# Reciprocal softmax sums repeated by DMA instead of TensorE, and one expert's down products ahead of the output projection

## The chip, the cores and the metric

The kernel runs on one core of a Trainium2 chip. The core has TensorE (PE, matrix products, into PSUM banks), VectorE (DVE), ScalarE (ACT), GpSimd (POOL) and SyncE (SP, which here issues DMAs); DMAs move data between HBM and the on-chip memory SBUF. Each engine runs its own list of instructions in order, and they wait for one another by semaphores. The metric is the device time of one execution in microseconds (us); lower is better. PE's clock has two levels, 1.2 and 2.4 GHz.

## What is computed

Two post-norm transformer layers on 16 sequences ("rows" of the batch) of 256 tokens and 128 features, all float32. In short:

```python
x = layernorm(x + attention0(rmsnorm(x)))   # 16 heads of 64; softmax over 256 keys; output projection + bias
x = layernorm(x + moe0(x))                  # 8 experts (hidden 256), top 2, plus one shared expert
x = layernorm(x + attention1(x))            # 16 tiny heads of 8, attention between the heads of one token
x = layernorm(x + moe1(x))                  # 8 experts (hidden 512), top 2
# attention0, per row of the batch and head:
weights = softmax(q @ k.T * Dh ** -0.5)     # exp(s - max) / sum of exps
out     = (weights @ v) @ w_out + b_out
```

The change concerns the division by the sum of exps in attention0.

## The kernel before

The 16 rows of the batch go through a software pipeline. Iteration `it` does attention0 and the first layer's up projections for row `it` (`v.a`), the rest of layer 0 and attention1 for row `it - 1` (`v.b`), and the second experts' down products and last norm for row `it - 2` (`v.c`). Weights are loaded once. Rows 0 and 1 run with a partly filled pipeline. Iterations 2 to 14 run as a hardware loop on every engine (`run`).

The order on PE is written out by hand in `pe_units`: a list of unit names with the PSUM bank of each. A bank has two semaphores: PE fills it (`v.fill(name)`), and whoever reads it last drains it (`v.drain(name)`); before PE starts a unit it waits until the previous unit of the same bank is drained. Banks S0/S1 take scores, T0/T1 transposed probabilities, A0/A1 alternate over QK, O, HT, OUT, V and X1T, and F0/F1 alternate over the fill units: down products D0p (layer 0) and D1e0 to D1e7 (layer 1, one expert each, 16 products in float32), and some small ones. By that alternation OUT takes the bank of O6, D1e6 the bank of D1e4 and D1e7 that of D1e5.

Attention0 of a row is a loop over 8 head pairs s:
- PE: scores S of pair s + 1, then O of pair s - 1 (values times probabilities, 64 + 64 output rows by 256 tokens), fill units, transposes T of pair s, QK of pair s + 3, fill units. After the loop: O7, the output projection OUT (32 products over all 8 pairs), D1e6, D1e7, V0, X1T (transposes of the normed sum), V1, V2 and the up projections U0 and U1 of the two layers.
- DVE: row maxima of each score bank (`head_max`, L711), the small part of QK (`lower_qk`), mixing of the down products into x (`mix`, L790), head attention of attention1 (L801 to L846), layer norms (L747 to L755), and for the division `inverse_sums` (L719) and `o_scale` (L724).
- ACT: the exponentials with row sums (`softmax_exp`, L573), copies out of PSUM (L552, L566), GELU (L594, L601), and for the division `o_out` (L561) and `repeat_inverse` (L625).
- POOL: norm roots (L446, L447) and half of attention1's products (L479 to L491).
- SP: one load of x (L381) and one store of the output (L421) per row; all weight loads at the start, the last of them (w1 and w2 among them) in `load_late`. w1 and w2 are 2 MB each.

The division: the exponentials' row sums stand one per partition (query token), but O is computed transposed, with tokens along the free dimension. So the reciprocals [128 tokens, 2 heads x 2 token tiles] are repeated by ACT to 64 columns per head (`row_inv`), transposed by PE with the identity into the other half of O's bank (`spread`, 2 transposes per pair), and DVE multiplies ACT's copy of O by them. PE runs `spread(s - 1)` ahead of the scores of pair s + 1, and for the last two pairs ahead of O itself. In `inverse_sums`, `settled` is a drain of the engine's pipeline.

## Time and profile before

| | us |
|---|---|
| median of 3 runs (lowest, highest) | 1432.32 (1432.04, 1434.01) |
| the profiled execution | 1431.51 |
| its span, first to last instruction | 1429.70 |
| PE busy | 1366.9 |
| DVE busy | 925.6 |
| ACT busy | 904.3 |
| POOL busy | 502.5 |
| mean granted PE clock, share of full | 0.988 |

All times in the profile are counted from the start of the span. Lnn is a line of the kernel. Busy time is the sum of the times in which an engine had an instruction in flight. A matmul's recorded duration is its latency in a pipeline, so several overlap; the time from one start to the next, or the piece it has in the chain of work that ended last, tells what it costs. An idle time in square brackets stands ahead of an instruction, with the instruction that released it.

### The profile page before, as it was taken

The numbers are of one execution on the slowest core, as the hardware profiler recorded it, in microseconds if no ns is written. First come the engines' busy times: TensorE is split into PE (matmuls) and PEld (weight loads), VectorE is DVE, ScalarE is ACT, GpSimd is POOL, SyncE is SP. The second block draws the span as 40 slices with busy tenths as digits, with TensorE's granted clock in tenths as the row PEclk, the third lists the DMA queues.
The fourth block names the chain that finished last, engine by engine and source line by source line (L and its number), as shares of the span: only waits on it lengthen the run. The fifth ranks groups of instructions, "written<-read, shape, count | busy, mean of one in ns | idle before, by whom it ended". The sixth has DMA issues, their size and how long they took to land.

```text
span 1429.7 us, 33458 instructions
## 1 busy us (share of the span) xinstructions
PE 1366.9 (96%) x11456; PEld 1202.2 (84%) x11456; DVE 925.6 (65%) x2535; ACT 904.3 (63%) x2492; POOL 502.5 (35%) x409
## 2 busy tenths in 40 slices
PE   6897999999999999999999999999999999999867
PEld 4685989888898988889898898988889898888767
DVE  4366576675766757566675757667576675756684
ACT  6675766757577575766657576675757657575423
POOL 3307062350705316071440706235070531607100
PEclk9999999999999999999999999999999999999988
DMA  7000000000000000000000000000000000000000
GB/s 262 5 1 5 1 2 8 0 7 0 0 7 0 7 0 0 7 0 7 0 7 0 0 7 0 7 0 7 0 0 7 0 7 0 0 5 1 5 1 8
DMA packets 13944, 13.77 MB, mean 10 GB/s; under 512 B 1609, under 2 KB 12754, under 8 KB 13650
## 3 DMA queue, kind: packets, MB, share of 16 engines
q1 hardware_dynamic: 13906, 13.27, 2.9%
q8 instruction: 23, 0.38, 0.1%
q14 instruction: 15, 0.12, 0.0%
HBM read 11.17 MB, written 2.10 MB: 9 GB/s over the span
## 4 chain that ended last, share of the span: by engine, by line
PE 64%; issue 11%; DVE 8%; ACT 4%; DVEq 4%; POOL 3%; POOLq 2%; SPq 1%; DMA 1%; ACTq 0%
PE bank_F L1208 14%; PE bank_S L1081 6%; DVEq L346 4%; PE bank_T L1067 4%; PE bank_T L1122 4%; PE bank_A L1135 4%; PE bank_T L1068 3%; PE bank_T L1069 3%; PE bank_F L1067 3%; ACT probs L573 3%; PE bank_F L1068 3%; PE bank_F L1069 3%; PE bank_A L1146 3%; PE bank_A L1067 3%; PE bank_A L1068 3%
## 5 line engine op out<-in xcount | busy, mean ns | idle before, releaser
L1208 PE MATMUL bank_F<-down,hid 128*128 128x128 f32 x2944 | 357.5, 277 | 5.4 <-DVE x L790 4.6
L1208 PEld LDWEIGHTS bank_F<-down,hid 128*128 128x128 f32 x2944 | 342.0, 192 | 14.7 <-DVE x L790 8.3
L573 ACT ACTIVATE probs<-bank_S,neg_max 128x256 f32<-128x256 f32 x512 | 236.2, 476 | 140.7 <-DVE neg_max L711 140.7
L711 DVE TENSOR_REDUCE neg_max<-bank_S 128x2 f32<-128x512 f32 x256 | 164.6, 684 | 96.1 <-PE bank_S L1081 96.0
L790 DVE SCALAR_TENSOR_TENSOR x<-bank_F,gates,x 128x128 f32<-128x128 f32 x496 | 149.8, 343 | 42.5 <-PE bank_F L1208 32.6
L491 POOL TENSOR_TENSOR hid<-hid,qkv 128x1024 f32<-128x1024 f32 x60 | 169.2, 2831 | 22.6 <-ACT hid L589 22.6
L461 POOL TENSOR_TENSOR mean_sq<-sum_sq,one_over_d 128x2 f32<-128x2 f32 x16 | 3.1, 197 | 442.8 <-ACT h_row L547 442.8
L552 ACT ACTIVATE probsT<-bank_T 128x512 f32<-128x512 f32 x256 | 139.6, 606 | 27.8 <-PE bank_T L1122 27.8
L479 POOL TENSOR_TENSOR hid<-qkv 128x1024 f32<-128x1024 f32 x45 | 121.1, 2690 | 69.3 <-ACT qkv L552 69.3
L1146 PE MATMUL bank_A<-probsT,values 128*64 128x256 f32 x1024 | 139.6, 394 | 1.1 <-ACT probsT L552 1.0
L1122 PE MATMUL bank_T<-ident,probs 128*128 128x128 f32 x1024 | 138.3, 278 | 0.2 <-ACT probs L573 0.2
L1122 PEld LDWEIGHTS bank_T<-ident,probs 128*128 128x128 f32 x1024 | 112.5, 141 | 25.4 <-issue 21.1
L1067 PE MATMUL bank_T<-x1T_hi,up_lo 128*128 128x256 f32 x442 | 129.4, 293 | 0.0
L601 ACT ACTIVATE hid<-bank_T 128x512 f32<-128x512 f32 x141 | 84.4, 598 | 63.6 <-PE bank_T L1069 53.7
L1068 PE MATMUL bank_T<-x1T_lo,up_hi 128*128 128x256 f32 x442 | 123.9, 280 | 0.0
L1069 PE MATMUL bank_T<-x1T_hi,up_hi 128*128 128x256 f32 x442 | 123.8, 280 | 0.0
L446 POOL TENSOR_TENSOR var_eps<-mv,ln_eps 128x2 f32<-128x2 f32 x64 | 12.6, 198 | 303.0 <-DVE mv L749 303.0
L1067 PE MATMUL bank_F<-x1T_hi,up_lo 128*128 128x256 f32 x358 | 103.8, 290 | 3.2 <-DVE x1T_lo L879 2.7
L573 ACT ACTIVATION_READ_ACCUMULATOR probs<-bank_S,neg_max 128x1 f32 x512 | 105.7, 206 | 0.0
L1069 PE MATMUL bank_F<-x1T_hi,up_hi 128*128 128x256 f32 x358 | 100.8, 281 | 0.0
L1068 PE MATMUL bank_F<-x1T_lo,up_hi 128*128 128x256 f32 x358 | 100.7, 281 | 0.0
L486 POOL TENSOR_TENSOR hid<-hid 128x512 f32<-128x512 f32 x75 | 95.3, 1270 | 10.7
(187 smaller groups left out, 3133.2 us busy)
## 6 DMA issues: line engine op xcount, KB each, us to landing
x_row<-in_x SPq DMA_DIRECT2D x16, 128.0 KB, 2.2
hid<-in_w SPq DMA_DIRECT2D x1, 2048.0 KB, 9.1
down<-in_w SPq DMA_DIRECT2D x1, 2048.0 KB, 14.3
out<-x SPq DMA_DIRECT2D x16, 128.0 KB, 1.8
hid<-in_rw SPq DMA_DIRECT2D x1, 1024.0 KB, 7.3
hid<-in_wv SPq DMA_DIRECT2D x1, 512.0 KB, 3.9
hid<-in_wq SPq DMA_DIRECT2D x1, 512.0 KB, 5.1
hid<-in_wk SPq DMA_DIRECT2D x1, 512.0 KB, 5.8
```

The lines of the kernel that those rows point to most:

```text
L479: settled(pool, g.tensor_tensor(prod[:, t, half(i)], q, k, ALU.mult))
L491: ins = g.tensor_tensor(pv1[:, t, half(i)], *weights_and_values(t, i), ALU.mult)
L552: sc.activation(dst, src, ACT.Copy).then_inc(v.drain(name)[0], 1)
L573: ins = sc.activation(probs[:, h // 2 % 2, h % 2, t, :], unit.bank(f"S{h}")[:, t * S:(t + 1) * S], ACT.Exp, bias=neg_max[:, h, t:t + 1], a ...
L711: ve.tensor_reduce(neg_max[:, h, :], v.bank(f"S{h}")[:, :].rearrange("p (t k) -> p t k", t=NT), AX.X, ALU.max, negate=True).then_inc(max_r ...
L790: ins = ve.scalar_tensor_tensor(acc[:, t, :], y[:, j, t, :], gates[i][:, t, e:e + 1], src[:, t, :], ALU.mult, ALU.add)
L1067: te.matmul(out, s_lo, m_hi, start=True, stop=False)
L1068: te.matmul(out, s_hi, m_lo, start=False, stop=False)
L1069: return te.matmul(out, s_hi, m_hi, start=False, stop=True)
L1122: ins = te.transpose(bank[:, k * S + t * P:k * S + (t + 1) * P], probs[:, h // 2 % 2, h % 2, t, tokens(k)], ident[:])
L1146: ins = te.matmul(bank[r, 0:S], values[:, k, s * P + j * DH:s * P + j * DH + DH], probsT[:, j, k, :], start=k == 0, stop=k == NT - 1)
L1208: ins = te.matmul(bank[:, (j * NT + t) * P:(j * NT + t + 1) * P], hid[:, e, k, tokens(t)], down[:, e, k, :], start=k == 0, stop=k == m - 1)
```

## The change

Two things. First, the reciprocals are no longer repeated on ACT and transposed on PE. DVE writes them into a tile padded to 32 columns, transposes it (each 32x32 block by itself), and SP stores the four blocks' first four rows to an HBM buffer `sums_apart` (four DMAs of 4 x 32 numbers), waits for them, and loads each head's row of 256 numbers back, repeated over 64 partitions (two DMAs), into `inv_spread`. DVE then multiplies O's bank by it directly; ACT's copy of O is gone. SP's loop is unrolled, and the loads of w1 and w2 move from SP's queue to ACT's, after ACT's work on pair 0 of row 0. DVE's transpose waits until SP's stores of the pair before have landed; SP's loads wait until `o_scale` of two pairs before is done, and its stores until the loads of the pair before have landed. Second, in PE's list D1e6 moves from behind OUT to ahead of it. DVE's order is the same. Small tiles `var_eps` and `std_inv` are merged into one each. The core of the diff:

```diff
@@ -46,6 +46,7 @@
 SPLIT1 = 8
 FIRST, LAST = 2, ROWS - 2
 LATE = 6
+SQ = 32
@@ -94,8 +95,10 @@
         put("A", f"QK{s + 3}", on=a and s + 3 < HP)
         put("A", "HT", on=nxt and s == HP - 2)
         put("F", *fill_units(it, s, 1))
-    put("A", f"O{HP - 1}", "OUT", on=a)
-    put("F", "D1e6", "D1e7", on=c)
+    put("A", f"O{HP - 1}", on=a)
+    put("F", "D1e6", on=c)
+    put("A", "OUT", on=a)
+    put("F", "D1e7", on=c)
     put("A", "V0", on=nxt)
     put("A", "X1T", on=a)
     put("G", "V1", on=nxt)
@@ -240,8 +243,10 @@
         probs = sb("probs", P, 2, 2, NT, S)
         probsT = sb("probsT", P, 2, NT, S)
         row_sum = sb("row_sum", P, 2, 2 * NT)
-        sum_inv = sb("sum_inv", P, 2, 2 * NT)
-        row_inv = sb("row_inv", P, 2, NT, 2, DH)
+        sum_inv = sb("sum_inv", P, SQ)
+        sum_invT = sb("sum_invT", P, SQ)
+        sums_apart = nc.dram_tensor("sums_apart", [2, 2 * NT, P], F32).ap()
+        inv_spread = sb("inv_spread", P, 2, S)
         oT_early = sb("oT_early", P, HP // 2, S)
         x1 = sb("x1", P, NT, D)
         x1T = split("x1T_hi", P, S), split("x1T_lo", P, S)
@@ -290,8 +295,9 @@
         stats = [sb(f"stats{i}", P, NT, 6) for i in range(4)]
         mv = [sb(f"mv{i}", P, NT, 2) for i in range(4)]
-        var_eps = [sb(f"var_eps{i}", P, NT) for i in range(4)]
-        std_inv = [sb(f"std_inv{i}", P, NT) for i in range(4)]
+        var_eps_all, std_inv_all = sb("var_eps", P, 4, NT), sb("std_inv", P, 4, NT)
+        var_eps = [var_eps_all[:, i, :] for i in range(4)]
+        std_inv = [std_inv_all[:, i, :] for i in range(4)]
         banks = {}
         for n in BANKS:
@@ -312,8 +318,8 @@
         h_ready = sem("h_ready")
         xplus_ready = sem("xplus_ready")
         inverse_ready = sem("inverse_ready")
-        repeated_ready = sem("repeated_ready")
-        o_copied = sem("o_copied")
+        inverse_stored = sem("inverse_stored")
+        inverse_spread = sem("inverse_spread")
         max_ready = sem("max_ready")
         stats_ready = [sem(f"stats_ready{i}") for i in range(4)]
@@ -361,7 +367,8 @@
             return (score1[:, t, half(i)].rearrange("p h (a g) -> p h a g", a=1).broadcast_to(full),
                     qkv1[:, t, :, 2, :].rearrange("p g (a d) -> p a d g", a=1).broadcast_to(full))
-        n_loads = [0] * 5
+        loads1 = (up1_loaded, w1_in), (down1[:], w2_in)
+        n_loads = [0, 0, 0, 0, 16 * len(loads1)]
         def wait_weights(eng, v, group):
@@ -406,8 +413,23 @@
                 load(3, wqkv1[:], wqkv1_in)
                 load(3, wproj[:], wproj_in)
                 load(4, router1[:], router1_in)
-                load(4, up1_loaded, w1_in)
-                load(4, down1[:], w2_in)
+
+            def spread_inverse(v, s):
+
+                sp.wait_ge(inverse_ready, v.at(0, HP, s + 1))
+                if v.it > 0 or s >= 1:
+                    sp.wait_ge(inverse_spread, v.at(0, 32 * HP, 32 * s))
+                for b in range(P // SQ):
+                    block = slice(b * SQ, (b + 1) * SQ)
+                    sp.dma_start(sums_apart[s % 2, :, block], sum_invT[block][0:2 * NT, :]).then_inc(inverse_stored, 16)
+                sp.wait_ge(inverse_stored, v.at(0, 64 * HP, 64 * (s + 1)))
+                if s >= 2:
+                    sp.wait_ge(*v.drain(f"O{s - 2}"))
+                elif v.it > 0:
+                    sp.wait_ge(*v.previous().drain(f"O{HP - 2 + s}"))
+                for j in range(2):
+                    src = sums_apart[s % 2, NT * j]
+                    sp.dma_start(inv_spread[j * DH:(j + 1) * DH, s % 2, :], bass.AP(src.tensor, src.offset, [[0, DH], [1, S]])).then_inc(inverse_spread, 16)
             def body(v):
                 if v.next:
@@ -416,11 +438,15 @@
                     load_x(v.it + 1 + v.step)
                 if v.it == 0:
                     load_late()
+                if v.a:
+                    for s in range(HP):
+                        spread_inverse(v, s)
                 if v.c:
                     sp.wait_ge(ln_ready[3], v.at(2, 1, 1))
                     sp.dma_start(out[v.it - 2 + v.step, :, :].rearrange("(t p) d -> p t d", p=P), x4[:]).then_inc(stored, 16)
-            run(sp, body)
+            for it in range(ROWS + 2):
+                body(Iteration(it, 0, banks))
             sp.wait_ge(stored, 16 * (ROWS + 1))
@@ -432,6 +458,7 @@
             g.affine_select(out=ident[:], in_=ident[:], compare_op=ALU.not_equal, fill=1.0, base=0,
                             pattern=[[-1, P]], channel_multiplier=1)
             g.memset(minus_half[:], -0.5)
+            g.memset(sum_inv[:], 0.0)
             g.memset(table_load[:], 0.0)
             for i in range(2):
                 g.memset(top2[i][:], -3.0e38)
@@ -555,11 +582,6 @@
                 t, half = n // 2, n % 2
                 copy_out(v, f"V{n}", values[:, t, half * 512:half * 512 + 512], v.bank(f"V{n}")[:, :])
-            def o_out(v, s):
-
-                act.wait_ge(*v.fill(f"O{s}"))
-                sc.activation(oT(s), v.bank(f"O{s}")[:, 0:S], ACT.Copy).then_inc(o_copied, 1)
-
             def qk_out(v, s):
                 act.wait_ge(*v.fill(f"QK{s}"))
@@ -618,12 +640,6 @@
                 sc.activation(table_load[:], table_load[:], ACT.Gelu)
                 for u in range(2 * E):
                     gelu1(v, u)
-
-            def repeat_inverse(v, s):
-
-                act.wait_ge(inverse_ready, v.at(0, HP, s + 1))
-                sc.activation(row_inv[:, s % 2], sum_inv[:, s % 2].rearrange("p (j t a) -> p t j a", j=2, a=1).broadcast_to([P, NT, 2, DH]),
-                              ACT.Copy).then_inc(repeated_ready, 1)
             def transposed_probs(v, s):
                 probsT_out(v, 2 * s)
@@ -643,8 +659,6 @@
                     router_exp(v, 1)
                 for s in range(HP):
                     if v.a and s == HP - 2:
-                        o_out(v, s - 1)
-                        repeat_inverse(v, s)
                         transposed_probs(v, s)
                     if v.a and s + 1 < HP:
                         softmax_exp(v, 2 * s + 2)
@@ -652,10 +666,6 @@
                         copy_out(v, "X2T", x2T[:], v.bank("X2T")[:, 0:S])
                     if v.a and s + 1 < HP:
                         softmax_exp(v, 2 * s + 3)
-                    if v.a and s >= 1 and s != HP - 2:
-                        o_out(v, s - 1)
-                    if v.a and s != HP - 2:
-                        repeat_inverse(v, s)
                     if v.b and s == 1:
                         copy_out(v, "WT0", gates0T, v.bank("WT0")[0:E + 1, 0:S])
                     if v.a and s != HP - 2:
@@ -665,14 +675,15 @@
                     if v.b and s == 3:
                         for t in range(NT):
                             copy_out(v, f"LQ{t}", qkv1[:, t].rearrange("p h c d -> p (h c d)"), v.bank(f"LQ{t}")[:, 0:3 * D])
+                    if v.it == 0 and s == 0:
+                        for dst, src in loads1:
+                            act.dma_start(dst, src).then_inc(loaded[4], 16)
                     if v.next and s == 1:
                         squares_of(v)
                     if v.b and s == 5:
                         head_exp(v, 0)
                 if v.b:
                     head_exp(v, 1)
-                if v.a:
-                    o_out(v, HP - 1)
                 sc.activation(table_load[:], table_load[:], ACT.Gelu)
                 if v.next:
                     for n in range(3):
@@ -716,12 +727,16 @@
                 unit = v.previous() if s == 0 else v
                 for j in range(2):
                     dve.wait_ge(*unit.drain(f"S{2 * s + j}"))
-                settled(dve, ve.reciprocal(sum_inv[:, s % 2, :], row_sum[:, s % 2, :]).then_inc(inverse_ready, 1))
+                settled(dve, ve.reciprocal(sum_inv[:, 0:2 * NT], row_sum[:, s % 2, :]))
+                if v.it > 0 or s >= 1:
+                    dve.wait_ge(inverse_stored, v.at(0, 64 * HP, 64 * s))
+                ve.transpose(sum_invT[:], sum_inv[:]).then_inc(inverse_ready, 1)
             def o_scale(v, s):
-                dve.wait_ge(o_copied, v.at(0, HP, s + 1))
-                ve.tensor_tensor(oT(s), oT(s), v.bank(f"O{s}")[:, S:2 * S], ALU.mult).then_inc(v.drain(f"O{s}")[0], 1)
+                dve.wait_ge(*v.fill(f"O{s}"))
+                dve.wait_ge(inverse_spread, v.at(0, 32 * HP, 32 * (s + 1)))
+                ve.tensor_tensor(oT(s), v.bank(f"O{s}")[:, 0:S], inv_spread[:, s % 2, :], ALU.mult).then_inc(v.drain(f"O{s}")[0], 1)
             def lower_qk(v, s):
@@ -1086,14 +1101,6 @@
             def whole_x3T(v):
                 return x3T_late if v.it == ROWS - 1 else x3T[:]
-
-            def spread(v, s):
-
-                bank = v.bank(f"O{s}")
-                pe.wait_ge(*v.drain(f"O{s}", before=1))
-                pe.wait_ge(repeated_ready, v.at(0, HP, s + 1))
-                for t in range(NT):
-                    te.transpose(bank[:, S + t * P:S + (t + 1) * P], row_inv[:, s % 2, t].rearrange("p j e -> p (j e)"), ident[:])
             def unit(v, name):
                 bank = v.bank(name)
@@ -1136,8 +1143,6 @@
                     return ins
                 if name[0] == "O":
                     s = int(name[1:])
-                    if s >= HP - 2:
-                        spread(v, s)
                     for j in range(2):
                         pe.wait_ge(*v.drain(f"T{2 * s + j}"))
                     for k in range(NT):
@@ -1223,8 +1228,6 @@
             def body(v):
                 for name, bank in (pe_units(v.it) if v.it >= 0 else PRE):
-                    if name[0] == "S" and bank == "S0" and v.nth.get(f"O{int(name[1:]) // 2 - 2}"):
-                        spread(v, int(name[1:]) // 2 - 2)
                     free, count = v.drain(name, before=1)
                     if v.it > 0 or count:
                         pe.wait_ge(free, count)
```

## Rows read from the trace of the kernel before

**Rows 1.** The page's first part: busy us, share of the span, instructions, by engine

```profile
PE 1366.9 (96%) x11456; PEld 1202.2 (84%) x11456; DVE 925.6 (65%) x2535; ACT 904.3 (63%) x2492; POOL 502.5 (35%) x409
```

**Rows 2.** Busy us by stage: stretch, its length, PE, PEld, DVE, ACT, POOL, clock

```profile
...
761.00:808.00 47.00, 46.77 (x409) 38.89 (x409) 32.55 (x80) 31.40 (x104) 22.70 (x16) 1.00 0.00 0
...
```

**Rows 3.** Timeline of PE (start, us, line, what), around OUT of a steady row

```profile
...
807.01 0.38 PE L1096 MATMUL bank_A<-ident,row_inv 128*128 128x128 f32 x2
...
808.61 2.05 PE L1135 MATMUL bank_A<-wo,oT_early 128*128 128x128 f32 x16 [0.21 <-DVE hid L724]
...
812.55 3.74 PE L1208 MATMUL bank_F<-down,hid 128*128 128x128 f32 x32
816.05 0.47 PE L1067 MATMUL bank_A<-wv_hi,hT_lo 128*128 128x512 f32 x1
...
816.82 0.38 PE L1051 MATMUL bank_A<-ident,x 128*128 128x128 f32 x2
...
```

**Rows 4.** Timeline of PE, behind OUT of row 15, which has no V0

```profile
...
1320.87 3.74 PE L1208 MATMUL bank_F<-down,hid 128*128 128x128 f32 x32
1324.96 0.41 PE L1051 MATMUL bank_A<-ident,x 128*128 128x128 f32 x2 [0.36 <-DVE x L755]
...
```

**Rows 5.** Instructions on row_inv and oT_early: ns least, median, most; first, last start

```profile
L1096 PE MATMUL bank_A<-ident,row_inv x256: 272/273/328, 24.5 to 1316.0; 128*128 128x128 f32 x128
L625 ACT ACTIVATE row_inv<-sum_inv x128: 404/433/446, 24.0 to 1312.3; 128x256 f32<-128x256 f32 x128
...
L561 ACT ACTIVATE oT_early<-bank_A x64: 392/395/407, 28.4 to 1298.1; 128x256 f32<-128x256 f32 x64
```

**Rows 6.** The chain that ended last (start, us, what), ahead of pair 6's scores

```profile
...
791.07 0.22 PE bank_A L1096 x2
...
```

**Rows 7.** Timeline of DVE in a steady row's attention

```profile
...
761.50 0.17 DVE L719 RECIPROCAL sum_inv<-row_sum 128x4 f32<-128x4 f32 x1
...
795.52 0.17 DVE L719 RECIPROCAL sum_inv<-row_sum 128x4 f32<-128x4 f32 x1
...
798.43 0.53 DVE L831 TENSOR_TENSOR hid<-hid,max 128x256 f32<-128x256 f32 x1
...
802.89 0.18 DVE L719 RECIPROCAL sum_inv<-row_sum 128x4 f32<-128x4 f32 x1 [1.89 <-ACT probs L573]
...
806.91 1.32 DVE L831 TENSOR_TENSOR hid<-hid,max 128x256 f32<-128x256 f32 x1
...
808.48 0.60 DVE L790 SCALAR_TENSOR_TENSOR x<-bank_F,gates,x 128x128 f32<-128x128 f32 x2
...
811.53 0.42 DVE L724 TENSOR_TENSOR hid<-hid,bank_A 128x256 f32<-128x256 f32 x1
...
```

**Rows 8.** DMAs: count, KB each, us to landing; one issue on SP

```profile
x_row<-in_x SPq DMA_DIRECT2D x16, 128.0 KB, 2.2
...
out<-x SPq DMA_DIRECT2D x16, 128.0 KB, 1.8
...
nscale<-in_norm_scale SPq DMA_DIRECT2D x1, 0.5 KB, 2.1
...
741.16 0.39 SPq L421 DMA_DIRECT2D out<-x  x1
```

**Rows 9.** Timeline of POOL beside the second L831 of rows 7

```profile
...
806.68 1.26 POOL L486 TENSOR_TENSOR hid<-hid 128x512 f32<-128x512 f32 x1
...
```

**Rows 10.** The chain that ended last, at the end of row 1's attention

```profile
...
129.03 5.53 POOL hid L491 x2
...
```

**Rows 11.** Row 0: last weight load (chain), DVE's first L719 and last L724

```profile
...
19.77 14.28 DMA down<-in_w
...
20.46 0.18 DVE L719 RECIPROCAL sum_inv<-row_sum 128x4 f32<-128x4 f32 x1 [1.47 <-ACT probs L573]
...
57.84 0.42 DVE L724 TENSOR_TENSOR hid<-hid,bank_A 128x256 f32<-128x256 f32 x1 [1.67 <-ACT hid L561]
...
```

**Rows 12.** Timeline of PE: X1T of row 0

```profile
...
64.64 0.66 PE L1051 MATMUL bank_A<-ident,x 128*128 128x128 f32 x2 [2.80 <-DVE x L755]
...
```

## The prediction

> **What bounds the kernel now.** I read the busy shares first: TensorE (PE) is busy 96% of the span [rows 1], so the question is where its instructions could start earlier. The busy time by stage says the same of one row's attention: 46.77 us of 47 [rows 2]. Then PE's own order of time at the end of that stage: in the stretch of rows 3 it stands still once, for 0.21 us, ahead of the output projection OUT, because VectorE (DVE) has not yet emptied the bank that OUT takes over from O6 [rows 3]. So a steady row (rows 2 to 14 of the batch, and nearly row 15) is PE-bound, but a second chain runs through DVE and ScalarE (ACT) in the last two head pairs and is only 0.2 us behind. After OUT the layer norm of x1 runs on DVE and GpSimd (POOL), and the transposes X1T need it. From the first matmul behind OUT to X1T go 816.82 - 812.55 = 4.27 us, filled by D1e6, D1e7 and V0 [rows 3]. In row 15 only D1e6 and D1e7 stand there, and X1T does wait 0.36 us: 1324.96 - 1320.87 = 4.09 us is what the norm needs [rows 4]. Its cover is thus 0.2 us too long, no more. Row 0 is another regime: its attention isn't PE-bound, and every delay there lengthens the run.
>
> **Parts of the change, on a steady row.**
> (a) `spread` goes: 256 transposes, in 128 pairs [rows 5]. Busy time overstates them (273 ns each); on the chain a pair takes 0.22 us [rows 6]. 8 pairs a row: 8 x 0.22 = 1.76 us of PE, 28 us over 16 rows if nothing else became late. That is the whole prize.
> (b) ACT loses `repeat_inverse` (0.433 us) and `o_out` (0.395 us) on each pair [rows 5]: 0.83 us, wherever ACT sets the pace.
> (c) DVE gains 8 transposes of 128x32 a row. No row shows one. Bounds: the reciprocal of four columns ahead of it, 0.17 us, and the product of 256 columns, 0.42 us [rows 7]. I take 0.2 us, being nearer to the small one. Six of the eight lie in DVE's idle time; two stand in the late chain. Less than nothing is impossible, as nothing is removed from DVE.
> (d) `o_scale` reads the bank directly instead of ACT's copy: same shape, so 0.42 us as before; it is free of ACT but waits for the DMA chain (e).
> (e) The DMA chain on the sync engine (SP) is strictly serial: wait for the reciprocals, four stores, wait for all four, two loads, and the next pair's stores wait for these loads. SP issues a DMA in 0.39 us; a store of 128 KB lands 1.8 us after its issue began, a load of 128 KB after 2.2 us, one of 4-byte pieces after 2.1 us [rows 8]. Stores: three issues of 0.3 to 0.43 us ahead of the last, then 1.6 us (an estimate, 1.8 less a little for the smaller size) to 1.8 = 2.5 to 3.1. Loads: one issue 0.43 ahead, then 2.1 us = 2.5. With 0.2 us for three wakes a round C is 5.2 to 5.8 us; I take 5.4. Bounds from the rows: 2 x 1.8 = 3.6 if all issues overlapped and 4 x 0.43 + 1.8 + 2 x 0.43 + 2.2 = 6.6 if none did.
> What the rounds must meet: the first reciprocal of the row is at 761.50 and `o_scale(7)` at 811.53 [rows 7], 50 us, against 8 x 5.4 = 43.2. There is a second, tighter condition: DVE's transpose for pair s waits until the stores of s - 1 have landed, and queued behind it on DVE are the whole head sums and maxima. For pair 6 (reciprocal at 795.52, about 1.4 us earlier after the change) this asks 761.7 + 5C + 0.53C < 794.1, that is C < 5.85 us. At 5.4 there are 2 us to spare. So in this case the DMA chain costs a steady row nothing; if the cover is gone, it costs 5.5 us per us of C.
> (f) D1e6 moves ahead of OUT. Its bank F1 is that of D1e4, so it can't start before DVE has mixed D1e4 (808.48 + 0.60 = 809.08 [rows 7]), which comes right behind `o_scale(6)`. How much earlier does DVE get there? PE reaches the scores of pair 6 5 x 0.22 = 1.1 us earlier (five spreads lie before). ACT's two instructions no longer stand between head_exp and the exponentials that the reciprocal at 802.89 waits for (1.89 us idle there [rows 7]): 0.6 to 0.8 us more. Against it two DVE transposes, 0.4. So DVE is 1.3 to 1.5 us early. There is a catch in either direction: the same subtraction L831 took 0.53 us at 798.43 and 1.32 at 806.91, ending 0.3 us after a POOL instruction that ended at 807.94 [rows 7, 9]; if it meets the gap between two POOL instructions instead, DVE is up to 2.6 us early. PE itself would be there 1.76 us early. D1e6 then starts 1.0 to 2.0 us before 808.61.
> From there: D1e6 1.75 us (half of 816.05 - 812.55), OUT 812.55 - 808.61 = 3.94, then the norm 4.09 before X1T, of which D1e7 and V0 cover only 1.75 + 0.77 = 2.5 [rows 3, 4]. PE now waits some 1.6 us at X1T. From D1e6's start to X1T 9.78 us, where OUT's start to X1T was 8.21: 1.57 us longer. Net a steady row gains 1.0 - 1.57 = -0.6 to 2.0 - 1.57 = +0.4 us; middle: 0.1 us lost. The 1.76 us that (a) frees turn into a wait at X1T. What D1e6 covers, `o_scale(7)`, which only the last four products of OUT need, wasn't late at C = 5.4. Times 14 rows: +1.4 us (-6 to +8).
> (g) Row 1 has no D1 products and is paced at its end by POOL, whose last two products end 129.03 + 5.53 = 134.56 and hold up the norm's root [rows 10]. POOL's series begins on LQ0, about 1 us earlier than now from three spreads and ACT's relief: -1 us.
> (h) Row 0. Before, 57.84 - 20.46 = 37.4 us from first reciprocal to `o_scale(7)` [rows 11], 4.8 a pair, less than a round. After, 8 x 5.4 = 43.2. Besides, the 4 MB of w1 and w2 go to ACT's queue about 7 us later than now (the last is issued at 19.77 and takes 14.28 us to land [rows 11]) and then cross the small transfers in some two rounds of four to six DMAs; I put 2 to 6 us on that, bounded below by none and above by the 14.28. Hidden: the OUT products before the last four, about 0.5 us. Sum 43.2 + 4 - 37.4 - 0.5 = +9, less 1 since ACT and PE are quicker at the end: +8 us (+2 to +14). POOL's splitting of w1 starts later too, but still ends before the norm.
> (i) Memset, merged small tiles, unrolled SP program: nothing on any chain; SP's waits between rows last tens of us.
>
> **Sum.** +1.4 - 1 + 8 = +8 us on a span of 1429.70. Outside the span lie 1431.51 - 1429.70 = 1.8 us, unchanged; the median of the runs is 0.8 above this execution. 1432.3 + 8 = 1440 us. Its own range by the bounds above: 1427 to 1454.
>
> **Rivals.**
> Rival 1, the DMA rounds set the pace (slower). For it: six issues and two landings of about 2 us are in series, and with the rows' full 0.43 and 1.8 C comes to 5.8 already. Against: the transfers are tiny. It decides from C = 5.85: at 6.2 the transpose of pair 6 stalls DVE 1.9 us, and OUT with it: 14 x 1.6 = +22, row 0 +14, so 1467 us. The Trainium skill (DMA: Bandwidth & Descriptors, Specifications and Anatomy of one DMA) speaks for this rival: pieces below 512 B are read, modified and written, and the receipt from HBM is the heaviest. The stores here are pieces of 128 B into HBM, and no run here shows one; by that rule a store lands later than the 1.8 us row, and the time is this rival's.
> Rival 2, the prize is kept (faster). The norm may be done sooner than row 15 shows, since POOL and DVE are both less loaded ahead of it, and D1e6 may start with PE's full 1.76 us: a row gains 1.2 us, 14 x 1.2 = -17, row 0 +5, row 1 -1: 1419 us. For it: 28 us of PE go, and PE is 96% busy. Against: 4.09 us of norm behind OUT are shown, and only 2.5 of cover stay.
> Rival 3, the clock. PE's transposes x2 took 0.66 us after an idle of 2.80 us in row 0, and 0.38 in a steady row [rows 3, 12]: the lower of its two levels. If the 1.6 us wait at X1T does that in each row, V1, V2 and X1T lose 1.4 us: 14 x 1.4 = +20, so 1460 us. Against: the idle is shorter and PE was full before.
>
> **How the numbers follow.** Forecast 0.50, rival 1 0.22, rival 2 0.20, rival 3 0.08. About 0.2% (2.9 us) is what a measurement can tell. Faster by more: rival 2 nearly whole, and a tenth of the forecast's spread: 0.25. Within: 0.15 of the forecast's half and a little of the rivals': 0.12. Slower: 0.63. For 8 in 10 the range runs from 1419, the centre of rival 2, to 1465, just short of rival 1's centre.
>
> **What would show it.** In the changed kernel's steady row: X1T with an idle of 1 to 2 us on DVE's ln_apply, D1e6 starting when D1e4 is mixed, no wait of `o_scale` for a DMA; reciprocals of row 0 at least 5.4 us apart. SP rounds near 5.4 us confirm (e); above 5.85 the DVE transpose waits for a DMA and rival 1 holds. If X1T doesn't wait, (f) is wrong and rival 2 holds. If row 0's OUT is not several us later, (h) is wrong. Matmuls of double length behind X1T mean rival 3.

## The result and the profile after

The changed kernel takes 1446.8 us (median of 4 runs, 1445.23 to 1447.92), against 1432.18 for the kernel before beside it (4 runs): a ratio of 1.0098, 95% interval 1.0083 to 1.0113. It is slower by 1%. The forecast was 1440.0 with a range of 1419 to 1465. The profiled execution took 1447.92 us, its span is 1446.1 against 1429.70, so 16.4 us are to be explained; mean granted clock 0.979 against 0.988.

The page's first part of the kernel after, to be held against [rows 1]:

```profile
PE 1352.1 (94%) x11200; PEld 1189.6 (82%) x11200; DVE 938.8 (65%) x2663; ACT 827.9 (57%) x2236; POOL 502.2 (35%) x410
```

PE lost 256 instructions and ACT 76 us of work; the time went up all the same. So the reading must go by the clock on the wall, with one mark for each row of the batch: the start of X1T, the transposes of the normed sum, on PE's timeline.

| | X1T of row 0 | row 1 after row 0 | row 2 after row 1 | a steady row | X1T of row 15 | span |
|---|---|---|---|---|---|---|
| before | 64.64 | 71.74 | 86.35 | 84.86 | 1324.96 | 1429.7 |
| after | 78.06 | 72.66 | 84.87 | 84.68 | 1336.60 | 1446.1 |

The 16.4 us are: row 0 +13.4; row 1 +0.9; the 14 rows to row 15's X1T together -2.7; and behind that X1T +4.8, of which 4.1 fall before the next transposes of x on PE (1351.06 against 1335.35).

**A steady row.** PE's timeline around OUT in the kernel after (start us, duration, line; the idle time ahead in brackets), where [rows 3] stood:

```profile
...
817.87 1.08 PE L1151 MATMUL bank_A<-probsT,values 128*64 128x256 f32 x8
818.88 2.05 PE L1213 MATMUL bank_F<-down,hid 128*128 128x128 f32 x16
820.77 1.95 PE L1142 MATMUL bank_A<-wo,oT_early 128*128 128x128 f32 x16
822.56 1.95 PE L1142 MATMUL bank_A<-wo,hid 128*128 128x128 f32 x16
824.34 1.95 PE L1213 MATMUL bank_F<-down,hid 128*128 128x128 f32 x16
826.05 0.48 PE L1082 MATMUL bank_A<-wv_hi,hT_lo 128*128 128x512 f32 x1
...
828.37 0.44 PE L1066 MATMUL bank_A<-ident,x 128*128 128x128 f32 x2 [1.39 <-DVE x L770]
...
```

No spread stands ahead of O7 any more, and D1e6 starts straight behind it. But from D1e7 to X1T go 828.37 - 824.34 = 4.03 us, the norm, and there is work only for the first 2.6: PE waits 1.39 us. This recurs in every steady row. PE's busy time by stage tells the same (stretch, length, then busy us and instructions of PE, PEld, DVE, ACT, POOL, the granted clock, the DMAs' share and GB/s). Before, then after:

```profile
250.00:1200.00 950.00, 944.90 (x8023) 834.39 (x8021) 633.59 (x1773) 626.00 (x1752) 349.69 (x278) 1.00 0.01 3
```

```profile
250.00:1200.00 950.00, 931.10 (x7868) 823.49 (x7867) 638.02 (x1859) 574.83 (x1563) 348.58 (x275) 1.00 0.05 15
```

**The rounds of the DMA chain.** SP's queue in the kernel after: L424 are the four stores, L432 the two loads. First row 0, then a steady row:

```profile
...
21.03 1.28 SPq L424 DMA_DIRECT2D sums_apart<-sum_invT  x4
23.21 1.15 SPq L432 DMA_DIRECT2D inv_spread<-sums_apart  x2
...
35.14 1.89 SPq L424 DMA_DIRECT2D sums_apart<-sum_invT  x4
37.92 1.09 SPq L432 DMA_DIRECT2D inv_spread<-sums_apart  x2
...
774.19 1.27 SPq L424 DMA_DIRECT2D sums_apart<-sum_invT  x4
776.34 1.09 SPq L432 DMA_DIRECT2D inv_spread<-sums_apart  x2
779.51 1.26 SPq L424 DMA_DIRECT2D sums_apart<-sum_invT  x4
...
```

A round is 779.51 - 774.19 = 5.32 us. In row 0 the first one takes 35.14 - 21.03 = 14.1 us: ACT issues the loads of w1 and w2 at 23.30 and 23.73, and pair 0's two loads of `inv_spread`, issued at 23.21 and 23.76, cross these 4 MB and land at 31.02 and 35.07 (w1 lands at 31.80, w2 at 38.12). DVE's waits for DMAs in the kernel after lie nearly all in row 0 (its timeline):

```profile
...
35.16 0.42 DVE L739 TENSOR_TENSOR oT_early<-bank_A,inv_spread 128x256 f32<-128x256 f32 x1 [8.03 <-DMA inv_spread<-sums_apart]
...
37.93 0.21 DVE L733 STREAM_TRANSPOSE sum_invT<-sum_inv 128x32 f32<-128x32 f32 x1 [2.25 <-DMA sums_apart<-sum_invT]
...
```

**Row 15.** It has no V0, and X1T waits 2.48 us instead of 0.36 [rows 4]. PE's timeline in the kernel after:

```profile
...
1336.60 0.41 PE L1066 MATMUL bank_A<-ident,x 128*128 128x128 f32 x2 [2.48 <-DVE x L770]
1338.26 0.55 PE L1082 MATMUL bank_F<-x1T_hi,up_lo 128*128 128x256 f32 x1 [1.25 <-DVE x1T_lo L894]
...
```

Behind it stands a stretch at the lower clock level (columns as above):

```profile
1336.60:1339.60 3.00, 1.75 (x8) 1.55 (x9) 2.69 (x7) 0.00 (x0) 0.00 (x0) 0.64 0.00 0
1339.60:1342.60 3.00, 3.00 (x16) 3.00 (x15) 1.86 (x3) 1.67 (x4) 0.00 (x0) 0.50 0.01 3
...
```

In the kernel before the granted clock is 1.00 in the same place, and 29 matmuls stand in 3 us (1328 to 1331) where 16 stand here.

### The profile page after: what moved, and what is told of

The parts are those of the page before. It is cut to its first block, busy times and chain, and to the rows that moved or that the text cites. A ratio compares the mean times of both kernels' runs of the same rounds, so it can differ in the third digit from the quotient of the medians.

```text
span 1446.1 us, 33731 instructions
## 1 busy us (share of the span) xinstructions
PE 1352.1 (94%) x11200; PEld 1189.6 (82%) x11200; DVE 938.8 (65%) x2663; ACT 827.9 (57%) x2236; POOL 502.2 (35%) x410
## 4 chain that ended last, share of the span: by engine, by line
PE 76%; issue 10%; DVE 5%; POOL 3%; DVEq 2%; POOLq 2%; DMA 1%; ACT 1%; SPq 0%; ACTq 0%
PE bank_F L1213 20%; PE bank_S L1096 7%; PE bank_A L1151 7%; PE bank_T L1129 6%; PE bank_T L1082 4%; PE bank_T L1083 3%; PE bank_T L1084 3%; PE bank_A L1142 3%; PE bank_F L1082 3%; PE bank_F L1083 3%; PE bank_F L1084 3%; PE bank_A L1082 3%; PE bank_A L1083 2%; PE bank_A L1084 2%; DVEq L352 2%
## 5 line engine op out<-in xcount | busy, mean ns | idle before, releaser
L1213 PE MATMUL bank_F<-down,hid 128*128 128x128 f32 x2944 | 361.2, 278 | 5.5 <-DVE x L805 4.6
L518 POOL TENSOR_TENSOR hid<-hid,qkv 128x1024 f32<-128x1024 f32 x60 | 168.9, 2825 | 11.3 <-ACT hid L611 11.3
L1082 PE MATMUL bank_T<-x1T_hi,up_lo 128*128 128x256 f32 x442 | 132.4, 300 | 0.0
L1151 PEld LDWEIGHTS bank_A<-probsT,values 128*64 128x64 f32 x1024 | 63.6, 138 | 49.8 <-DVE oT_early L739 6.8
## 6 DMA issues: line engine op xcount, KB each, us to landing
down<-in_w ACTq DMA_DIRECT2D x1, 2048.0 KB, 14.4
```

The lines of the kernel that those rows point to most:

```text
L518: ins = g.tensor_tensor(pv1[:, t, half(i)], *weights_and_values(t, i), ALU.mult)
L1082: te.matmul(out, s_lo, m_hi, start=True, stop=False)
L1151: ins = te.matmul(bank[r, 0:S], values[:, k, s * P + j * DH:s * P + j * DH + DH], probsT[:, j, k, :], start=k == 0, stop=k == NT - 1)
L1213: ins = te.matmul(bank[:, (j * NT + t) * P:(j * NT + t + 1) * P], hid[:, e, k, tokens(t)], down[:, e, k, :], start=k == 0, stop=k == m - 1)
```

## Experiments

The theory of the forecast, called A below: the DMA chain (5.3 us a round) costs a steady row nothing, taking `spread` away gains, D1e6 ahead of OUT uncovers the norm behind OUT and eats the gain, and row 0 loses by the rounds and by their crossing of the 4 MB.

### The two halves alone

`e1_order_back`, the kernel after with the old order on PE:

```diff
-    put("A", f"O{HP - 1}", on=a)
-    put("F", "D1e6", on=c)
-    put("A", "OUT", on=a)
-    put("F", "D1e7", on=c)
+    put("A", f"O{HP - 1}", "OUT", on=a)
+    put("F", "D1e6", "D1e7", on=c)
```

> The changed kernel with D1e6 behind OUT again, as in the kernel before; the DMA chain stays. Theory A (the order gives back what the removed transposes free): the wait at X1T (1.39 us in a steady row) goes, a steady row takes 83.2 to 83.4 us instead of 84.68, row 15 keeps the high clock (some 4 us), and the median is about 1422 us, below both kernels. Theory B (the DMA chain eats the gain, and D1e6 covers it): OUT's last four products wait for o_scale(7), a steady row takes 84.7 us or more, and the median is 1446 us or higher.

Measured: 1421.92 us, ratio to before 0.9911 (0.989 to 0.9933). A steady row takes 82.9 us. PE's timeline of it around OUT:

```profile
...
808.61 2.05 PE L1140 MATMUL bank_A<-wo,oT_early 128*128 128x128 f32 x16
...
812.28 3.74 PE L1211 MATMUL bank_F<-down,hid 128*128 128x128 f32 x32
...
816.56 0.38 PE L1064 MATMUL bank_A<-ident,x 128*128 128x128 f32 x2
```

OUT follows O7 without a wait, and so does X1T: the norm is covered. The row is 0.3 us shorter than expected, and one part of the expectation failed: row 15 does not keep the high clock (13.39 us from its X1T to the next transposes of x, 10.39 in the kernel before).

`e2_order_alone`, the kernel before with the new order alone (the same lines the other way round):

> The kernel before with D1e6 ahead of OUT, nothing else. Theory A: D1e6 starts when D1e4 is mixed, 0.5 us behind OUT's old start, and X1T follows 9.8 us later instead of 8.2, so a steady row takes 86.5 to 86.9 us instead of 84.87 and the median is 1455 to 1465 us. Theory B: the order costs nothing by itself, 84.9 us a row and 1432 us.

Measured: 1459.13 us, ratio 1.0175 (1.0157 to 1.0194); a steady row 86.8 us. PE's timeline:

```profile
...
823.69 2.05 PE L1210 MATMUL bank_F<-down,hid 128*128 128x128 f32 x16 [0.71 <-DVE x L792]
825.58 1.95 PE L1137 MATMUL bank_A<-wo,oT_early 128*128 128x128 f32 x16
...
833.06 0.44 PE L1053 MATMUL bank_A<-ident,x 128*128 128x128 f32 x2 [1.26 <-DVE x L757]
```

What follows: the two halves pull against each other. The division by DMA takes 84.86 - 82.9 = 1.96 us from a steady row, the new order adds 84.68 - 82.9 = 1.8 (on the kernel before 86.8 - 84.86 = 1.9). Over the whole run the order costs 25 us (1446.8 - 1421.9; 1459.1 - 1432.9 = 26 on the kernel before).

### Is the DMA chain felt in a steady row?

`e4_no_dma`: the kernel after without SP's stores and loads and without the waits for them. `inv_spread` holds a constant, so the division is left out.

```diff
-                if v.a:
-                    for s in range(HP):
-                        spread_inverse(v, s)
...
+            g.memset(inv_spread[:], 0.01)
```

> The changed kernel without the whole DMA chain: no stores, no loads, no waits on them; o_scale multiplies by a constant tile instead of the reciprocals, so the softmax division is left out. DVE still computes and transposes the reciprocals. Theory A: the steady row is the same, 84.6 to 84.7 us, with X1T waiting 1.4 us; only row 0 is shorter, by 13 to 17 us, and the median is 1428 to 1434 us. Theory B: the steady row falls to 83.5 us or less and the median to below 1420.

Measured: 1428.29 us, ratio 0.9955 (0.9939 to 0.997); a steady row 84.70 us with 1.26 us of wait at X1T; X1T of row 0 at 59.94, row 1 70.79. The chain costs a steady row nothing (84.68 with it), 18.1 us in row 0 (a little more than the 13 to 17 expected) and 1.9 in row 1; row 2 gives 2.3 of it back (87.12 against 84.87), which was not followed.

`e7_double_stores`: each store is made twice, the second time into a buffer that nobody reads; eight stores a round.

```diff
+                    sp.dma_start(sums_again[s % 2, :, block], sum_invT[block][0:2 * NT, :]).then_inc(inverse_stored, 16)
...
-                sp.wait_ge(inverse_stored, v.at(0, 64 * HP, 64 * (s + 1)))
+                sp.wait_ge(inverse_stored, v.at(0, 128 * HP, 128 * (s + 1)))
```

> The changed kernel with every store of the reciprocals issued twice (a second HBM buffer takes the extra ones), so that a round takes 6.6 us instead of 5.33; nothing else. The prediction's rival 1 (a round above 5.85 us holds DVE's transpose of pair 6 and with it OUT): a steady row grows by 3.5 to 4.5 us to about 88.7, row 0 by 10, the median is 1500 to 1520 us. If the rounds aren't near any limit: steady rows stay at 84.7, the median is 1457.

Measured: 1538.2 us, ratio 1.0744 (1.0717 to 1.0771); steady rows of 88.9 to 90.8 us, 89.6 on average. SP's queue and DVE's timeline of this run:

```profile
...
829.57 1.27 SPq L425 DMA_DIRECT2D sums_again<-sum_invT  x4
...
836.23 1.26 SPq L425 DMA_DIRECT2D sums_again<-sum_invT  x4
...
```

```profile
...
866.63 0.21 DVE L737 STREAM_TRANSPOSE sum_invT<-sum_inv 128x32 f32<-128x32 f32 x1 [2.15 <-DMA sums_apart<-sum_invT]
...
883.20 0.42 DVE L743 TENSOR_TENSOR hid<-bank_A,inv_spread 128x256 f32<-128x256 f32 x1 [2.24 <-DMA inv_spread<-sums_apart]
...
```

With a round of 6.66 us both waits that the forecast named for rival 1 are there: DVE's transpose stands behind the stores of the pair before, and `o_scale(7)` behind its loads. 4.9 us a row are lost; the forecast's rule (nothing up to 5.85, then 5.5 us per us) gives 0.81 x 5.5 = 4.5. TensorE's clock has a part in it, too: the mean granted clock is 0.960 against 0.979, and ten of the 13 rows have a stretch at the lower level; the three without one (89.50, 88.96 and 88.90 us) lose 4.4 on average. The median is above the 1500 to 1520 expected, since row 2 (94.55 us) and row 1 (79.93 against 72.66) lose more than the steady rows.

`e11_double_back`: the same with the old order on PE.

> Edit: e7_double_stores (eight stores a round instead of four, so a round of 6.65 us, steady rows of 88.9 to 90.8 us) with D1e6 behind OUT, as in the kernel before. Theory A (in e7 the cost of D1e6 ahead of OUT is still there, since the wait at X1T is still 1.38 us): the rows get 1.2 to 1.4 us shorter and the median is about 1518. Theory B (with rounds of 6.65 us the chain of DMAs sets the row, and the place of D1e6 only moves a wait from X1T to OUT): the rows stay, and the median is within 5 us of 1538.

Measured: 1531.57 us, ratio 1.0673 (1.0653 to 1.0694). The steady rows average 89.5 us, as in `e7_double_stores`, and PE now waits at the last products of OUT instead of at X1T:

```profile
...
881.39 0.71 PE L1144 MATMUL bank_A<-wo,hid 128*128 128x128 f32 x4 [1.47 <-DVE hid L741]
...
```

Theory B holds for the rows: with rounds this long the chain sets the row, and the place of D1e6 only chooses where PE waits. The median fell by 6.6, beyond B's 5 but far from A's 20: 2.8 us of it stand in front of row 15's X1T, 2.2 behind it, the rest lies between the profiled executions and the medians. So D1e6 ahead of OUT costs 1.8 us a row just because the chain is short enough not to matter.

### Row 0: the crossing with the weight loads

`e3_late_w`: w1 and w2 are issued by ACT at pair 7 of row 0 instead of pair 0, and POOL's split of w1 comes after row 0's norm.

```diff
-                    if v.it == 0 and s == 0:
+                    if v.it == 0 and s == HP - 1:
```

> The changed kernel with the loads of w1 and w2 issued after ACT's pair 7 of row 0 instead of pair 0, and POOL's splitting of w1 moved behind x_plus of row 0, so that it isn't waited for by the first norm. Theory A (row 0's loss of 13.4 us is the first two loads landing in 11.3 us beside w1 and w2, then rounds of 5.3 us): the first loads land in 2.6 us, all rounds of row 0 are 5.3 to 5.5 us apart, X1T of row 0 starts near 69 us instead of 78.06, and the median falls by 8 to 10 us to about 1438. Theory C (row 0 is late because of the split of w1 on POOL or the lower clock, not the transfers): X1T of row 0 stays within 3 us of 78 and the median within 3 us of 1446.

Measured: 1447.95 us, ratio 1.0098 (1.0081 to 1.0116), no different from the kernel after. The collision had only moved: X1T of row 0 comes at 77.46, and SP's queue shows which round was hit:

```profile
...
59.94 1.39 SPq L424 DMA_DIRECT2D sums_apart<-sum_invT  x4
68.44 1.09 SPq L432 DMA_DIRECT2D inv_spread<-sums_apart  x2
...
```

8.5 us instead of 2.15 from the stores to the loads. The run says nothing on the size of the loss in the kernel after; the edit had to take the loads past the last round. `e5_later_w` does, at ACT's copy of V0, behind all rounds of row 0:

```diff
-                    if v.it == 0 and s == 0:
-                        for dst, src in loads1:
-                            act.dma_start(dst, src).then_inc(loaded[4], 16)
...
+                        if v.it == 0 and n == 0:
+                            for dst, src in loads1:
+                                act.dma_start(dst, src).then_inc(loaded[4], 16)
```

> As e3_late_w, but the loads of w1 and w2 are issued by ACT behind V0 of row 0, when all transfers of row 0 have landed (in e3 they ran into pair 7's). The order is that of the changed kernel. Theory A: no load of the reciprocals takes over 3 us, X1T of row 0 starts at 69 to 71 us, the median is 1438 to 1440 us. Theory C (row 0 is held by something else): X1T of row 0 within 3 us of 78, median within 3 us of 1447.

Measured: 1449.44 us, ratio 1.012 (1.0099 to 1.0141). Row 0's X1T does come 8.3 us earlier (69.8), but row 1 takes 83.54 us instead of 72.66. `e6_back_later`, the same with the old order:

> e5_later_w with D1e6 behind OUT again. Theory A: the two gains add, a steady row takes 82.9 us and row 0 is 8 us shorter than in e1: 1413 to 1415 us. If the new place of the split of w1 on POOL or of the loads disturbs row 1, up to 1420.

Measured: 1423.03 us, ratio 0.9934 (0.991 to 0.9958): row 0 70.4 (`e1_order_back` 78.68, so again 8.3 us), row 1 83.64 (72.72), steady rows 82.87. The crossing costs 8.3 us. (The edit also takes POOL's split of w1 out of row 0; but beside that split, 49.20 to 61.82 in the kernel after, no instruction of DVE is longer than elsewhere in the row.) Row 1 then took it back and 2.6 us more. The expectation of `e6_back_later` had named the split's new place as a risk, up to 1420; the loss was larger, and its mechanism was in no theory.

DVE's and POOL's timelines of `e5_later_w` in row 1 show it:

```profile
...
83.48 1.93 DVE L777 COPY top<-top 128x4 f32<-128x4 f32 x1
...
86.08 8.29 DVE L780 TENSOR_TENSOR shifted<-logits,top 128x16 f32<-128x16 f32 x1
```

```profile
81.78 3.60 POOL L480 CAST up_hi<-hid 128x4096 fp32r<-128x4096 f32 x1 [11.32 <-DMA down<-in_w]
85.53 8.81 POOL L483 TENSOR_TENSOR up_lo<-hid,up_hi 128x4096 fp32r<-128x4096 f32 x1
```

A subtraction of 16 columns, 0.18 us in the kernel after, takes 8.29 us and ends at 94.37, with POOL's subtraction of 4096 columns (94.34). Both have two operands in SBUF. That became theory D. In `e3_late_w` the split has the same place in POOL's list, but its loads had landed and it ran from 78.07 to 90.83, ahead of the router's instructions on DVE (91.47, 0.17 us); row 1 took 72.99 us. So it is the meeting that costs, and not the split in row 1 as such.

### Taking the serial rounds apart, and testing theory D

`e8_two_sems`: `e6_back_later` with two semaphores for the loads, by even and odd pair, so that a pair's stores need not wait for the loads of the pair before.

```diff
-                if v.it > 0 or s >= 1:
-                    sp.wait_ge(inverse_spread, v.at(0, 32 * HP, 32 * s))
+                if v.it > 0 or s >= 2:
+                    sp.wait_ge(inverse_spread[s % 2], v.at(0, 16 * HP, 32 * (s // 2)))
```

> e6_back_later with two semaphores in turn for the loads of the reciprocals, so that the stores of a pair wait for the loads of two pairs before, not of the pair before. Theory A (row 0 is paced by rounds of 5.3 us): the rounds of row 0 shrink to the 4.4 to 4.8 us that the engines need, X1T of row 0 starts at 62 to 65 us, steady rows stay at 82.9 us, the median is 1405 to 1409 us. If something else paces row 0: no change against e6_back_later.

Measured: 1413.01 us, ratio 0.9864 (0.9846 to 0.9883). Row 0's X1T comes at 59.23, 11.2 us earlier than in `e6_back_later` and earlier than the 62 to 65 expected; steady rows stay at 82.87. The median missed the expected 1405 to 1409 by 4 us; row 1's loss (83.76 us) is still in it. SP's queue in row 0:

```profile
...
20.58 1.28 SPq L422 DMA_DIRECT2D sums_apart<-sum_invT  x4
22.75 1.15 SPq L430 DMA_DIRECT2D inv_spread<-sums_apart  x2
24.32 1.26 SPq L422 DMA_DIRECT2D sums_apart<-sum_invT  x4
...
28.06 1.50 SPq L422 DMA_DIRECT2D sums_apart<-sum_invT  x4
...
```

The stores of the next pair now start 0.4 us after the loads are issued, and a pair takes 3.7 us at first, and at most 4.0 up to pair 6.

`e9_w1_early`: w1's load back at pair 0 and POOL's split of it back in row 0; w2's load stays late, with a semaphore of its own.

```diff
+                    if v.it == 0 and s == 0:
+                        act.dma_start(*loads1[0]).then_inc(loaded[4], 16)
...
-                            for dst, src in loads1:
-                                act.dma_start(dst, src).then_inc(loaded[4], 16)
+                            act.dma_start(*loads1[1]).then_inc(w2_loaded, 16)
```

> Edit: e8_two_sems with w1's load (2 MB) at row 0's pair 0, w2's load (2 MB) at V0 as before in e8, and GpSimd's split of w1 back where the kernel after has it, in row 0's course; TensorE waits for w2 by a semaphore of its own before D1 of row 1. The two loads of 4 MB thus no longer stand together beside the rounds, and the split no longer falls into row 1. Theory D (row 1's loss of 10.9 us in e8, X1T to X1T 83.76 us against 72.66 in the kernel after, is GpSimd's split of the 128x4096 weights holding VectorE's work on the router's logits in row 1): row 1 goes back to 72 to 73 us, row 0's X1T comes at 61 to 67 (the rounds beside 2 MB instead of 4), the steady rows stay at 82.9, and the median is 1404 to 1409. Theory L (row 1's loss comes from where the loads run): row 1 stays over 80 us and the median over 1412.

Measured: 1411.8 us, ratio 0.9839 (0.9822 to 0.9857). Row 1 is back at 72.82 us: the loss of 10.9 us had not come with w2's late load. The median missed the forecast of 1404 to 1409, since row 0 gave 7.7 us of it back (66.97 against 59.23) and row 2 another 1.4.

`e10_pieces`: `e8_two_sems` with the split in 16 pieces of 256 columns, in the same place.

```diff
+                        for j in range(2):
+                            part = slice(j * 256, (j + 1) * 256)
+                            g.tensor_copy(w_hi[:, e, part], whole[:, e, part])
+                            pool.drain()
+                            ins = g.tensor_tensor(w_lo[:, e, part], whole[:, e, part], w_hi[:, e, part].bitcast(F32), ALU.subtract)
```

> Edit: e8_two_sems with GpSimd's split of w1 (cast, subtract) in 16 pieces of 128x256 in the place that it has in e8; the same work, shorter instructions. Theory D (VectorE's small instruction on two SBUF operands took 8.29 us in e5_later_w because it stood behind one running instruction of GpSimd): with pieces of about 0.6 us each such instruction waits for one piece at most; row 1 (X1T to X1T) is 74 to 78 us instead of 83.76, and the median 1404 to 1407. If the loss is the total of GpSimd's work, or something that the pieces do not change, row 1 stays at 83 to 84 and the median at 1413.

Measured: 1404.67 us, ratio 0.979 (0.977 to 0.981), the fastest version here. Row 1 takes 74.43 us, though POOL does the same work, 18.1 us of it instead of 12.4. DVE's subtraction of 16 columns:

```profile
...
76.59 0.53 DVE L788 TENSOR_TENSOR shifted<-logits,top 128x16 f32<-128x16 f32 x1
...
```

Theory D holds: what counts is the length of the one POOL instruction that DVE's instruction meets. Row 2 gave 2.7 us back; I did not look for its cause.

### Row 15 and the clock

`e12_last_row_back`: the kernel after with the old order in row 15 alone.

```diff
+    if nxt:
+        put("F", "D1e6", on=c)
+        put("A", "OUT", on=a)
+    else:
+        put("A", "OUT", on=a)
+        put("F", "D1e6", on=c)
```

> Edit: the kernel after, with D1e6 behind OUT in row 15 alone (rows 0 to 14 keep D1e6 ahead of OUT). After row 15's X1T the granted clock is 0.5 for 9.3 us in the kernel after and for 7.2 us in e1_order_back, where TensorE had waited 2.48 and 0.70 us at X1T; from this X1T to the next transposition of x there are 14.46 us in after, 13.39 in e1_order_back and 10.39 in before (no such stretch, wait 0.36). Theory C (the part of the low clock that goes beyond e1_order_back's comes from the 2.48 us wait, thus from D1e6 ahead of OUT in row 15): the wait is 0.70, X1T comes 1.8 us earlier, the distance is 13.4 instead of 14.46, and the span 2.9 us shorter than after's 1446.1, 1443.2. Theory N (that part has another cause): the distance stays 14.46 and the span is 1444.3, only the 1.8 us shorter. Both leave open why e1_order_back has a low stretch at all and before none.

Measured: 1442.81 us (5 runs), ratio to before 1.0073 (1.0059 to 1.0087), span 1442.5. PE's timeline:

```profile
...
1334.58 0.41 PE L1070 MATMUL bank_A<-ident,x 128*128 128x128 f32 x2 [0.69 <-DVE x L774]
...
1347.95 0.41 PE L1070 MATMUL bank_F<-ident,x 128*128 128x128 f32 x2 [0.64 <-DVE x L774]
```

X1T is 2.0 us earlier, and the distance to the next transposes is 13.37 us instead of 14.46. These are the numbers of theory C, but other traces speak against its cause. PE's timeline of `e3_late_w`, which has the order and the wait of the kernel after:

```profile
...
1338.64 0.41 PE L1065 MATMUL bank_A<-ident,x 128*128 128x128 f32 x2 [2.48 <-DVE x L769]
...
1352.02 0.41 PE L1065 MATMUL bank_F<-ident,x 128*128 128x128 f32 x2 [0.63 <-DVE x L769]
```

The wait is the same 2.48 us and the distance 13.38. All traces, each one execution of its version:

| wait at row 15's X1T | distance to the next transposes of x |
|---|---|
| 2.48 | 14.46 after, 14.4 `e5_later_w`, 13.38 `e3_late_w`, 13.37 `e7_double_stores` |
| 2.15 | 13.38 `e2_order_alone`, 13.38 `e4_no_dma` |
| 0.69 or 0.70 | 13.4 in `e1_order_back`, `e8_two_sems`, `e9_w1_early`, `e10_pieces` and `e12_last_row_back`; 11.97 `e6_back_later`, 10.45 `e11_double_back` |
| 0.36 | 10.39 before |

So the order in row 15 is shown to cost 2.0 us ahead of X1T. The 1.1 us of clock do not follow from the longer wait, and the length of the wait alone does not decide whether the clock falls: 0.70 us stand before 13.4 as well as before 10.45. Why it falls, and how far this differs between executions of one kernel, stays open.

## Why the prediction was right, and where its terms were off

**Right.** The sign and the reason for it. (a) and (b): the division by DMA takes 1.96 us from a row when nothing else becomes late, against 1.76 in the sum. (c): the transpose takes 0.211 us (128 of them), against 0.2. (e): a round is 5.32 us, against 5.4, and the steady row doesn't feel it (`e4_no_dma`); the stores land some 2.15 us after the first issue began, issues included, which is below the 2.5 to 3.1 of the sum, while the loads take 2.6. Rival 1's condition, rounds over 5.85, was of the right size as far as `e7_double_stores` tells, which tried the one value of 6.66. The Trainium skill's rule that pieces below 512 B are read, modified and written (DMA: Bandwidth & Descriptors, Specifications) spoke for that rival: a store should have landed later than the 1.8 us row. The trace does not bear that out: the stores of 128 B pieces are landed 0.9 us after the fourth issue ended. Whether larger pieces would land sooner still, no run here shows. (f): D1e6 to X1T took 828.37 - 818.88 = 9.49 us (9.78 in the sum) and started 9.49 - 8.21 + 0.18 = 1.5 us earlier in the row than OUT had (1.0 to 2.0, middle 1.5): net -0.18 us a row, against +0.1 with ends of -0.4 and +0.6 in the same sense. The 14 rows thus gave 2.7 us where the sum's middle had lost 1.4. The wait at X1T is 1.39, against 1.6. Rival 2 would have needed that wait to be near zero; it is what `e1_order_back` makes, by another way.

In the gap of POOL, too, the forecast's catch was real. DVE's and POOL's timelines in the kernel after:

```profile
...
817.45 0.42 DVE L846 TENSOR_TENSOR hid<-hid,max 128x256 f32<-128x256 f32 x1
...
```

```profile
...
814.67 2.85 POOL L518 TENSOR_TENSOR hid<-hid,qkv 128x1024 f32<-128x1024 f32 x1
817.65 1.34 POOL L513 TENSOR_TENSOR hid<-hid 128x512 f32<-128x512 f32 x1
```

L846 is the L831 of [rows 7]. It met the gap and took 0.42 us instead of 1.32.

**Off: step (h), row 0.** +13.4 us against +8, at the upper end of its 2 to 14. The term that failed is the crossing with the 4 MB, put at 2 to 6 us, 4 in the sum: it is 8.3 (`e6_back_later` against `e1_order_back`), since pair 0's loads took 11.3 us to land and every later round stands in series behind them. That explains 4.3 of the 5.4 us; without the crossing row 0 is 69.80 - 64.64 = 5.2 us later (`e5_later_w`), where the sum without it gives 4.3. The bound was in the rows (the 14.28 us of [rows 11]); I took a value at the foot of it because the transfers are small. But the two loads, issued within 0.1 us of the long ones, took 7.8 us beside w1's 8.5 and 11.3 us beside w2's 14.4, where 2.6 us is the median. The forecast was also wrong in when the 4 MB start: 4.0 us later than before (w2 at 23.73 against 19.77), not 7.

**Off: step (g), row 1.** +0.9 us against -1. The catch of step (f) was not applied to this row. DVE's timeline of row 1 in the kernel after, then PE's:

```profile
...
138.41 2.03 DVE L846 TENSOR_TENSOR hid<-hid,max 128x256 f32<-128x256 f32 x1
140.36 0.41 DVE L739 TENSOR_TENSOR hid<-bank_A,inv_spread 128x256 f32<-128x256 f32 x1
...
```

```profile
...
140.83 3.78 PE L1142 MATMUL bank_A<-wo,oT_early 128*128 128x128 f32 x16 [3.20 <-DVE hid L739]
...
```

Here L846 met a POOL instruction that ran until 140.15, `o_scale(6)` came behind it, and OUT waited 3.20 us and then ran at the lower clock (16 products in 3.78 us; 2.05 in [rows 3]). POOL's timeline of the kernel after shows that POOL no longer sets the end of this row:

```profile
...
141.52 5.58 POOL L518 TENSOR_TENSOR hid<-hid,qkv 128x1024 f32<-128x1024 f32 x2
148.90 0.20 POOL L473 TENSOR_TENSOR var_eps<-mv,ln_eps 128x2 f32<-128x2 f32 x1 [1.80 <-DVE mv L764]
...
```

Its series ends 147.10 - 78.06 = 69.04 us behind row 0's X1T, against 134.56 - 64.64 = 69.92 before: the 1 us that the forecast had. But X1T follows 3.62 us behind it instead of 1.82, since the norm now waits for OUT. That is the whole difference of 1.9 us.

The same shape stands in `e4_no_dma` (OUT waits 2.84 us), whose row 1 is 1.9 us shorter than with the chain. Of these, 1.5 us are there by row 1's first scores (13.46 us behind row 0's X1T, 11.97 in `e4_no_dma`). Directly behind row 0's X1T the granted clock is at the lower level in the kernel after and at the upper one in `e4_no_dma` (columns as above, the kernel after first):

```profile
78.06:81.28 3.22, 3.22 (x9) 2.64 (x10) 0.85 (x2) 0.60 (x1) 0.66 (x1) 0.50 0.15 46
```

```profile
59.94:63.16 3.22, 3.22 (x23) 2.95 (x23) 0.85 (x2) 1.86 (x4) 0.67 (x1) 1.00 0.17 46
```

**Off: row 15.** +4.1 us behind its X1T were in no term. Rival 3 had named the mechanism, a lower clock after a longer wait, but priced it for all rows: in the 14 rows with 1.39 us of wait the clock stays at 1.00 (the stage of 250 to 1200 us above), and only row 15, where nothing but D1e7 covers the norm, falls. The 4.1 us stay open: the traces show the lower clock in them, but not what decides it.

Sum: 13.4 + 0.9 - 2.7 + 4.8 = 16.4 us, against 8 - 1 + 1.4 = 8 in the forecast (both rounded). Row 0, row 1 and what lies behind row 15's X1T came out 12 us above their terms together, and the steady rows 4 us below theirs: the range held because it was wide, and a part of the errors cancelled.

## What to carry to other kernels

Cover behind a step is a budget like time on an engine: before moving work ahead of a step to hide one latency, measure what that work hides where it stands. Here D1e6 hid 1.4 us of norm behind OUT and nothing ahead of it, and moving it turned a gain of 0.9% into a loss of 1%. A serial chain of small transfers that a steady stage hides completely still sets the pace of the first, half-filled iteration: keep long transfers out of its way, and let its rounds overlap (11 us of row 0 and 10 us of the median here, for one more semaphore).

## Hardware behaviour that I had not expected

An instruction of VectorE with two operands in SBUF was held by the GpSimd instruction in flight, however small it was itself: 16 columns took 8.29 us beside a GpSimd subtraction of 8.81 us, 0.53 us beside pieces of 0.73 us, and 0.18 us in the kernel after. The wait is recorded as its own duration and not as idle time, so that it hides in "busy"; one reads it off from an end that coincides with GpSimd's. The Trainium skill has this as a rule: the pair of ports that the two share is an exclusive lock, held for the whole instruction (SBUF — State Buffer, SBUF: two separate sides). The page counts a float32 copy from SBUF to SBUF among the instructions that take the pair, and the traces agree there too: the copy of 4 columns (L777, 1.93 us, 0.17 us in the kernel after) ended at 85.41, GpSimd's cast at 85.38. By that rule the forecast could have asked for row 1, too, which GpSimd instruction L831 would meet.
